# Router of a language-model kernel: the base rows move from VectorE to ScalarE, the root's inputs from GpSimd to VectorE

## Reference

```python
h = weight[x]                                   # token rows
h = h + attention(layernorm(h))                 # 16 heads, rotary terms
n = layernorm(h)                                # (h - mean) / sqrt(var + 1e-5)
probs = softmax(n @ w_router)                   # 32 experts, top 1
slot = expert * C + position of the token among its expert's, if below C = 320
y = expert(n)                                   # silu(n w_gate) * (n w_up) @ w_down
out = h + (n + y * gate)                        # the second n is the ffn block's own residual
```

## Time and profile before

| | |
|---|---|
| runs | 3315.01 us median of 3 (3313.55 to 3324.78) |
| profiled execution | 3315.87 us, span 3314.0 us |
| stage C | from 2914 to 3064 us of the span |
| PE / DVE / ACT / POOL busy over the span | 97% / 88% / 74% / 17% |
| mean granted TensorE clock | 0.986 of full speed |

### The profile page before, as it was taken

One profiled execution on the slowest core, in us unless ns is written; L12 is line 12 of the kernel. 1 busy time (PEld: TensorE's weight loads), 2 busy tenths in 40 slices (PEclk: granted clock), 3 DMA queues, 4 the chain that ended last, 5 costly groups with the idle time before them and its releaser, 6 DMA issues.

```text
span 3314.0 us, 67613 instructions
## 1 busy us (share of the span) xinstructions
PE 3202.7 (97%) x27520; PEld 1369.7 (41%) x27520; DVE 2908.6 (88%) x3157; ACT 2468.7 (74%) x4578; POOL 565.3 (17%) x752
## 2 busy tenths in 40 slices
PE   7997999999999999999999999999999999986999
PEld 3443333333333333333333333333333333365666
DVE  6889999999999999999999999999999999567222
ACT  3331888888888888888888888888888888943221
POOL 7882000000000000000000000000000000046233
PEclk9997999999999999999999999999999999998999
DMA  6895213131313131313131313122222220168773
GB/s 201 256 299 159 54 49 72 37 72 37 72 38 72 38 74 38 72 40 72 37 72 39 83 34 79 39 70 44 65 45 58 45 83 21 37 204 305 231 238 101
DMA packets 269155, 305.40 MB, mean 92 GB/s; under 512 B 45270, under 2 KB 198399, under 8 KB 265517
## 3 DMA queue, kind: packets, MB, share of 16 engines
q1 hardware_dynamic: 256812, 271.63, 29.7%
q0 software_dynamic: 12032, 29.45, 2.7%
HBM read 165.81 MB, written 139.23 MB: 92 GB/s over the span
## 4 chain that ended last, share of the span: by engine, by line
PE 81%; ACT 4%; DVE 3%; issue 2%; POOL 1%; DMA 0%; another core or an unknown queue 0%; SPq 0%; POOLq 0%; DVEq 0%
PE ps_o L916 33%; PE ps_s L899 26%; PE ps_m L868 13%; ACT probs L1012 2%; PE ps_g L1592 2%; PE ps_y L1603 2%; PE ps_u L1592 2%; DVE max_parts L1027 2%; ACT weighted L992 1%; PE ps_td L1581 1%; ACT rows_c L1343 1%; POOL slot_rows L1257 0%; PE ps_s L883 0%; POOL shift_c L1234 0%; DVE stats_c L1377 0%
## 5 line engine op out<-in xcount | busy, mean ns | idle before, releaser
L1027 DVE TENSOR_REDUCE max_parts<-ps_m 128x2 f32<-128x1024 f32 x2048 | 2486.1, 1223 | 79.9 <-PE ps_m L868 71.5
L1012 ACT ACTIVATE probs<-ps_s 128x512 f32<-128x512 f32 x4096 | 2217.5, 597 | 312.3 <-PE ps_s L899 127.8
L868 PE MATMUL ps_m<-keys,queries 48*128 48x512 f32 x4096 | 1483.5, 453 | 17.1 <-DVE max_parts L1027 16.7
L899 PE MATMUL ps_s<-queries,keys 51*128 51x512 f32 x4096 | 1480.5, 447 | 9.5 <-ACT probs L1012 3.1
L916 PE MATMUL ps_o<-probs,vals 128*32 128x256 f32 x16384 | 1295.5, 391 | 0.0
L899 PEld LDWEIGHTS ps_s<-queries,keys 51*128 51x128 f32 x4096 | 610.5, 185 | 832.2 <-issue 785.2
L868 PEld LDWEIGHTS ps_m<-keys,queries 48*128 48x128 f32 x4096 | 595.4, 187 | 77.4 <-DVE max_parts L1027 50.2
L916 PEld LDWEIGHTS ps_o<-probs,vals 128*32 128x32 f32 x16384 | 329.4, 108 | 720.4 <-issue 699.0
L824 POOL TENSOR_TENSOR heads_out<-weighted,recip_rows 128x512 f32<-128x512 f32 x63 | 80.9, 1285 | 2147.4 <-DMA recip_rows<-recip_rows_dram 2147.4
L1663 DVE TENSOR_TENSOR hidden<-ps_u,silu 128x320 f32<-128x320 f32 x64 | 31.5, 492 | 127.4 <-PE ps_u L1592 101.6
L1639 ACT ACTIVATE silu<-ps_g 128x320 f32<-128x320 f32 x64 | 28.0, 438 | 134.1 <-PE ps_g L1592 82.8
(11 more groups left out here) (108 smaller groups left out, 1600.0 us busy)
## 6 DMA issues: line engine op xcount, KB each, us to landing
slot_rows<-empty SPq DMA_DIRECT2D x16, 1290.0 KB, 5.2
vext<-val SPq DMA_DIRECT2D x64, 256.0 KB
halves_q<-parts SPq DMA_DIRECT2D x64, 256.0 KB
halves_k<-parts SPq DMA_DIRECT2D x64, 256.0 KB
keys<-halves_k SPq DMA_DIRECT2D x32, 512.0 KB, 7.5
queries<-halves_q SPq DMA_DIRECT2D x128, 128.0 KB, 3.2
vals<-vext SPq DMA_DIRECT2D x32, 512.0 KB, 5.6
recip_rows<-recip_rows_dram SPq DMA_DIRECT2D x64, 256.0 KB
```

The costliest lines, as they stand in the source:

```text
L868: mm = pe.matmul(ps_m[m % 2][:, h, :], queries_r[par][rows, qt, p, t * P:(t + 1) * P], keys_r[par][rows, p, c * 512:(c + 1) * 512], start= ...
L899: pe.matmul(ps_s[bank][:], keys_r[par][rows, p, k * P:(k + 1) * P], queries_r[par][rows, qt, p, :], start=True, stop=True).then_inc(scores ...
L1012: act.activation(probs[:, n % RING, :], ps_s[bank][:], ACT.Exp, scale=SCALE).then_inc(probs_ok[bank], 1)
L1027: dve.tensor_reduce(max_parts[:, lu % 2, :, p, t, c], ps_m[m % 2][:], AX.X, ALU.max).then_inc(maxima_ok[m % 2], 1)
```

## The change

1. Router, DVE: `base` is gone. After the gate, DVE makes `neg_mean` and `var_eps` by two `tensor_scalar` on 128x4 (`root_inputs`); the moments now come before the gate.
2. Router, ACT: a new `base` of four activations `resid * (rstd + 1) + shift`, which is `h + n`. It follows `normalise` of the next chunk.
3. Router, POOL: `root` loses `var_eps` and `neg_mean` and gains `rstd_one` = `rstd` + 1. The wait for the base rows stands ahead of `root`.
4. Router, DVE: since ACT now reads `resid` for the base, `residual` of chunk c + 2 waits until the base of chunk c is written.
5. Stage A: DVE makes `neg_mean` and `var_eps`, between the two `sums`; POOL's `root` loses them.

```diff
 (stage A)
@@ gpsimd, root
-                pool.wait_ge(stats_ok, after(b, k, CT))
-                pool.tensor_tensor(var_eps[:, k, :], mv[:, k, :, 1], eps_sb[:], ALU.add).then_inc(eps_ok, 1)
-                pool.tensor_tensor(neg_mean[:, k, :], no_mean[:], mv[:, k, :, 0], ALU.subtract).then_inc(neg_mean_ok, 1)
                 pool.wait_ge(eps_ok, after(b, k))
@@ vector
+            def root_inputs(b, k):
+                dve.wait_ge(stats_ok, after(b, k, CT))
+                dve.tensor_scalar(neg_mean[:, k, :], mv[:, k, :, 0], -1.0, None, ALU.mult)
+                dve.tensor_scalar(var_eps[:, k, :], mv[:, k, :, 1], EPS, None, ALU.add).then_inc(eps_ok, 1)
...
                 dve.tensor_tensor(sums[:, 1, 0, :], terms[:, 1, 0, :], terms[:, 1, 1, :], ALU.subtract).then_inc(sums_ok[1], 1)
+                if ahead:
+                    root_inputs(*ahead)
                 dve.tensor_tensor(sums[:, 1, 1, :], terms[:, 1, 2, :], terms[:, 1, 3, :], ALU.add).then_inc(sums_ok[1], 1)
 (router)
@@ sync, chunk
-                sp.wait_ge(base_ok, after(b, k))
+                sp.wait_ge(base_ok, after(b, k, CT))
@@ gpsimd, root
-                pool.wait_ge(stats_ok, after(b, k, CT))
-                pool.tensor_tensor(var_eps[:, k % 2, :], mv[:, k % 2, :, 1], eps_sb[:], ALU.add).then_inc(eps_ok, 1)
-                pool.tensor_tensor(neg_mean[:, k % 2, :], no_mean[:], mv[:, k % 2, :, 0], ALU.subtract).then_inc(neg_mean_ok, 1)
...
                 pool.tensor_tensor(shift[:, k % 2, :], neg_mean[:, k % 2, :], rstd[:, k % 2, :], ALU.mult).then_inc(shift_ok, 1)
+                pool.tensor_tensor(rstd_one[:, k % 2, :], rstd[:, k % 2, :], ones_c[:], ALU.add).then_inc(rstd_one_ok, 1)
@@ gpsimd, chunk
+                pool.wait_ge(base_ok, after(b, k, CT))
                 if not (last and k + 2 >= CPB):
                     root(*nxt(b, k, 2))
-                pool.wait_ge(base_ok, after(b, k))
@@ scalar
+            def base(b, k):
+                act.wait_ge(rstd_one_ok, after(b, k))
+                for t in range(CT):
+                    act.activation(rows[:, k, t, DM:2 * DM], resid[:, k % 2, t, :], ACT.Identity, bias=shift[:, k % 2, t:t + 1],
+                                   scale=rstd_one[:, k % 2, t:t + 1]).then_inc(base_ok, 1)
...
                     normalise(*nxt(b, k, 2))
+                if not (last and k == CPB - 1):
+                    base(*nxt(b, k))
 
             normalise(0, 0)
             copy_t(0, 0)
             normalise(0, 1)
+            base(0, 0)
@@ vector, residual
+                if (b, k) not in ((0, 0), (0, 1)):
+                    dve.wait_ge(base_ok, after(b, k, CT) - 2 * CT)
@@ vector
-            def base(b, k):
-
-                dve.wait_ge(norm_ok, after(b, k, CT))
-                dve.tensor_tensor(rows[:, k, :, DM:2 * DM], resid[:, k % 2], rows[:, k, :, 0:DM], ALU.add).then_inc(base_ok, 1)
+            def root_inputs(b, k):
+                dve.wait_ge(stats_ok, after(b, k, CT))
+                dve.tensor_scalar(neg_mean[:, k % 2, :], mv[:, k % 2, :, 0], -1.0, None, ALU.mult)
+                dve.tensor_scalar(var_eps[:, k % 2, :], mv[:, k % 2, :, 1], EPS, None, ALU.add).then_inc(eps_ok, 1)
@@ vector, chunk
+                if more:
+                    row_moments(*n)
                 gate(b, k)
                 if more:
-                    row_moments(*n)
+                    root_inputs(*n)
                 counts(b, k)
                 own(b, k)
                 slots(b, k)
-                if not (last and k == CPB - 1):
-                    base(*nxt(b, k))
```

More of the change, by code:

```diff
@@ L229, in phase_a @@
         neg_half = sb("neg_half", [P, CT])
-        eps_sb = sb("eps_sb", [P, CT])
-        no_mean = sb("no_mean", [P, CT])
         neg_mean = sb("neg_mean", [P, 4, CT])
@@ L255, in phase_a @@
         eps_ok = sem("eps_ok")
-        neg_mean_ok = sem("neg_mean_ok")
         rstd_ok = sem("rstd_ok")
@@ L368, in root @@
                 pool.wait_ge(rstd_ok, after(b, k))
-                pool.wait_ge(neg_mean_ok, after(b, k))
                 pool.tensor_tensor(shift[:, k, :], neg_mean[:, k, :], rstd[:, k, :], ALU.mult).then_inc(shift_ok, 1)
             pool.memset(neg_half[:], -0.5).then_inc(half_set, 1)
-            pool.memset(eps_sb[:], EPS).then_inc(half_set, 1)
-            pool.memset(no_mean[:], 0.0).then_inc(half_set, 1)
-            pool.wait_ge(half_set, 3)
+            pool.wait_ge(half_set, 1)
             for k in range(2):
@@ L569, in _ @@
             dve.memset(val[:], 1.0).then_inc(ones_set, 1)
-            row_stats(0, 0)
-            dve.wait_ge(stats_raw, CT)
-            row_moments(0, 0)
-            row_stats(0, 1)
-            dve.wait_ge(stats_raw, 2 * CT)
-            row_moments(0, 1)
+            for k in range(2):
+                row_stats(0, k)
+                dve.wait_ge(stats_raw, (k + 1) * CT)
+                row_moments(0, k)
+                root_inputs(0, k)
             dve.wait_ge(const_in, 16 * NCONST)
@@ L1108, in phase_c @@
         w_o, w_router, expert_no = router.w_o, router.w_router, router.expert_no
-        neg_half, eps_sb, no_mean, carry = router.neg_half, router.eps_sb, router.no_mean, router.carry
+        neg_half, carry = router.neg_half, router.carry
         token_no, att_t, emb = router.token_no, router.att_t, router.emb
@@ L1117, in phase_c @@
         shift = sb("shift_c", [P, 2, CT])
+        rstd_one = sb("rstd_one", [P, 2, CT])
+        ones_c = sb("ones_c", [P, CT])
         rows = sb("rows_c", [P, CPB, CT, ROW])
@@ L1149, in phase_c @@
         eps_ok = sem("eps_ok_c")
-        neg_mean_ok = sem("neg_mean_ok_c")
         rstd_ok = sem("rstd_ok_c")
         shift_ok = sem("shift_ok_c")
+        rstd_one_ok = sem("rstd_one_ok")
         norm_ok = sem("norm_ok_c")
@@ L1232, in root @@
                 pool.wait_ge(rstd_ok, after(b, k))
-                pool.wait_ge(neg_mean_ok, after(b, k))
                 pool.tensor_tensor(shift[:, k % 2, :], neg_mean[:, k % 2, :], rstd[:, k % 2, :], ALU.mult).then_inc(shift_ok, 1)
+                pool.tensor_tensor(rstd_one[:, k % 2, :], rstd[:, k % 2, :], ones_c[:], ALU.add).then_inc(rstd_one_ok, 1)
             pool.memset(neg_half[:], -0.5).then_inc(half_set, 1)
-            pool.memset(eps_sb[:], EPS).then_inc(half_set, 1)
-            pool.memset(no_mean[:], 0.0).then_inc(half_set, 1)
-            pool.wait_ge(half_set, 6)
+            pool.memset(ones_c[:], 1.0).then_inc(half_set, 1)
+            pool.wait_ge(half_set, 3)
             pool.wait_ge(proj_ps, 1)
@@ L1451, in _ @@
                 row_moments(0, k)
-            base(0, 0)
+                root_inputs(0, k)
             dve.wait_ge(carry_set, 1)
```

2 lines of the change are left out of this document (removed).

## The result

| | before | after |
|---|---|---|
| median of 6 runs each | 3314.28 us (3311.21 to 3324.78) | 3335.2 us (3332.89 to 3351.98) |
| profiled execution | 3315.87 us, span 3314.0 | 3332.89 us, span 3331.1 |
| mean granted TensorE clock | 0.986 | 0.983 |
| first stage, up to the last `full` | 284.1 | 284.4 |
| attention, up to the router's first residual add | 2634.2 | 2633.5 |

The ratio of the changed kernel to the one before is 1.007, with the interval 1.0049 to 1.009: slower, as forecast. Nearly all of it lies in the router, 16.8 of the 17.1 us between the two spans. The stage lengths are read from timelines of VectorE and TensorE.

A forecast was written before the change was run, and what follows sets the result against it. The router was taken as bound by a turn of waits, 8.04 us a chunk, becoming 9.30. Router 16.4 + 2.0 - 0.6 = 17.8 plus first stage 2.2 gave 20.0 us more: 3335.0 us, range 3325 to 3346.

The forecast's parts named there:

- The ring: Router, one turn a chunk: residual add, root inputs, GpSimd root, ScalarE normalisation and base, next residual add; 9.30 us against 8.04.
- Step 1: Router, VectorE from the start of the residual add through statistics, gate, moments and the two new instructions: 3.68 us.
- Step 2: Router, hand-over by semaphore from VectorE to GpSimd: 0.10 us, an estimate.
- Step 3: Router, GpSimd from the start of `rstd` to ScalarE's start: 1.35 us.
- Step 4: Router, ScalarE's eight activations in a row, normalising and base: 4.07 us.
- Step 5: Router, hand-over from ScalarE back to VectorE: 0.10 us.
- 13 x 1.26 = 16.4: Router, 13 turns, each longer by 9.30 - 8.04 us: 16.4 us more.
- The start: Router start: from the moments of chunk 1, the residual add of chunk 2 comes 2.0 us later.
- The end: Router end: last normalisation starts 5.13 us after its residual add instead of 5.70, 0.6 us back; the tail keeps its length.
- The first stage: First stage: two small VectorE instructions between the sums of the keys cost 0.16 us in each of 14 chunks, 2.2 us.
- Rival A: Router: the new wait does not bind, turn 7.50 us through the exponentials; 3310.2 us, no change to tell; chance 0.12.
- Rival B: Router: TensorE falls to its low clock and stays there, turn 11.5 us, 28.6 us more, 3363.6 us; chance 0.08.

The follow-up runs named there:

- second traces: The unchanged kernel before and the changed kernel each run and profiled once more: 3313.15 us and 3334.47 us, one run each.
- The doses: Changed kernel with two extra ScalarE activations a chunk, before (3362.13 us) or after the base rows (3343.19), or with half the residual add waiting for two rows (3325.93).
- dose in the ring: Changed kernel with two more activations a chunk on ScalarE, unused results, ahead of the four base activations: 3362.13 us, ratio 1.0142 to the kernel before.
- dose beside the ring: Changed kernel with two more activations a chunk on ScalarE, unused results, after the base rows and ahead of the copy: 3343.19 us, ratio 1.0093.
- router alone: Changed kernel with the first stage as before, its two small root inputs back on GpSimd: 3337.38 us, ratio 1.0068 to the kernel before.
- Inputs alone: Kernel before with only the router's root inputs made by VectorE, moments ahead of the gate, base add still on VectorE: 3313.32 us, ratio 0.9999.
- three buffers: Changed kernel with a third residual buffer, so the residual add of chunk c + 2 waits for the base of chunk c - 1: 3321.99 us, ratio 1.0019.
- base early: Changed kernel with ScalarE's base of chunk c + 1 ahead of the normalisation of chunk c + 2: 3320.29 us, ratio 1.0016 to the kernel before.

## Why the prediction was right

3335.0 us was forecast, 3335.2 measured. That the two agree to 0.2 us is luck: the spans of the two profiled executions lie 17.1 us apart, those of the second traces 21.5, and the medians 20.9. By its own steps:

- **The bound** was read rightly as a turn and not as the engine with the largest busy share. VectorE's busy share fell from 14.42 of 16 us to 12.71 of 18.56 and the stage became longer.
- **The ring.** Step 1, 3.68: measured 3.66. Step 2, the hand-over to GpSimd, 0.10: measured 0.15. Step 3, 1.35: 1.35. Step 4, 4.07: 4.04. Step 5, 0.10: 0.09. Sum 9.30 forecast, 9.29 in the turn shown, 9.28 as the mean of 13. The doses moved it by what they should. The wait itself was forecast as about 2.5 us in each of chunks 2 to 15; it is so in nine of them and smaller in five.
- **13 x 1.26 = 16.4.** The other side of the difference is less firm than it looked. The second trace of the kernel before has 7.87 us in nearly every turn and not 8.58 and 7.44 by turns, so the steady part costs 16.1 us in the first pair of traces and (9.31 - 7.89) x 13 = 18.5 in the second.
- **The start, +2.0.** From the moments of chunk 1 to the residual add of chunk 2 the changed kernel takes 2931.36 - 2925.17 = 6.19 us, against 4.21 in the earlier trace rows: 1.98 more. The mechanism is right, but in the first trace most of it was given back: the projection of chunk 1 ran at full clock there and the moments came earlier. TensorE, changed kernel, first trace:

```profile
2919.27 3.69 PE L1264 MATMUL ps_p<-w_o,att_t 128*128 128x256 f32 x16 [2.50 <-DVE resid L1375]
```

  and second trace:

```profile
2918.59 5.38 PE L1264 MATMUL ps_p<-w_o,att_t 128*128 128x256 f32 x16 [2.51 <-DVE resid L1375]
```

  In both traces of the kernel before it took 5.38. The granted clock from 2918 to 2926 us was 1.00 in the one and 0.79 in the three others, after the same idle time of 2.5 us. From the first residual add to that of chunk 2 the traces have 13.21 (before, twice), 13.51 and 15.19 (changed): +0.3 and +2.0. All 14 traces agree. The 16 matmuls took 3.69 us in seven of them and 5.29 to 5.38 in the other seven. Nine traces, in which the residual add of chunk 2 starts without a wait for base rows, have 13.2 us from the one add to the other with either. With the wait (and no dose in the ring) there are two more, 13.50 behind matmuls of 3.69 (dose beside the ring) and 15.17 behind the longer kind (router alone). So the term was right for a start with the longer matmuls, which the traced kernel before had, and 1.7 too high for the other.
- **The end, -0.6.** The last normalisation starts 3057.20 - 3052.04 = 5.16 us after its residual add, forecast 5.13, before 5.70. The logits of chunk 15 start at 3062.41, 3.14 us after that normalisation ended, as in the earlier trace rows.
- **Router together, +17.8:** measured +16.8 and +21.1, mean 19.0. With the first stage's 0.8, below, that makes 19.8 against 20.0 forecast; a router term 1.2 too small and a first-stage term 1.4 too large cancel, which is luck again.
- **The first stage, +2.2, was too high.** VectorE's first `sums` of the keys, changed kernel:

```profile
56.36 2.10 DVE L591 TENSOR_TENSOR sums<-terms 128x512 f32<-128x512 f32 x1
...
153.11 2.11 DVE L591 TENSOR_TENSOR sums<-terms 128x512 f32<-128x512 f32 x1
172.27 2.11 DVE L591 TENSOR_TENSOR sums<-terms 128x512 f32<-128x512 f32 x1
```

  Six spacings from 56.36 to 153.11 are 16.12 us each, where the kernel before has 16.00: 0.12 and not 0.16. The next is 19.16 where it was 19.55, since a transfer sets it, and the last two stages of the 14 do not have the step at all. From that block to the last one, the nine traces with this first stage have 223.7 to 225.3 us, the five without it 222.9 to 224.1: +0.8 on average. The term should have been some 0.8. Two of the 14 steps were none, the others 0.13 and not 0.16, and the spacing that a transfer sets gave 0.6 back (19.2 on average against 19.8), so the rival within the sum, that transfers swallow it, held for that part.
- **`shift`** took 0.19 to 0.20 in every chunk and not 0.85, and no base add of VectorE stands beside it now. Inputs alone shows how fine this is: `shift` took 0.21 us in the chunks where it started 0.06 ahead of the base add, and 1.27, up to the end of that add, in the three where it started 3 to 5 ns behind it. **`own_place`** took 0.29 beside a running `rstd` (2990.93, `rstd` from 2990.86 to 2991.90). The rule of the Trainium skill, page "SBUF — State Buffer", section "Who interferes with whom", would have it wait for the end of `rstd`, which issued first; the row does not show that, and neither does any other of the 14 chunks in which the two overlap. Nothing in the ring hung on it.
- **Rival A** did not come: the wait bound in all 14 chunks. Its consequence was tested by the kernels that took the wait away. Its price was 7.50 us a turn and no win. With three buffers the turns without a long wait for a load take 6.8 to 7.8 us, three of them 7.31; the means of 7.5 to 8.0 hold the late loads too. The time was the same as before or up to 0.2% longer.
- **Rival B** did not come. TensorE stood 2.00 us ahead of the projections and kept full clock in most turns. The low level appeared for single stretches. VectorE's slack took those that left the clock of a turn at 0.82, as the text said, but not the longer ones: behind a turn at 0.65 the next took 9.67 (changed kernel, second trace), and a turn at 0.54 took 10.06 (router alone). That is this rival in single turns, 0.4 to 0.9 us each, and 1.6 once with the dose in the ring. The Trainium skill, page "TensorE: Matmul & The Clock Gate", section "Why this matters for your kernels", advises against idle gaps between bursts of matmuls, and means longer ones than were needed here: the turn at 0.54 began with 2.00 us of idle TensorE, as did turns at full clock, and in the kernel with base early 2.54 us of waiting for a load was followed by 8 us at 0.50.

VectorE's share, 12.71 of 18.56, is 10.96 of 16, where some 11 was said.

## What to carry to other kernels

Moving work to an idle engine helps only if no ring that it comes to lie in gets longer than the present turn. Whoever lets another engine read a buffer gives the writer of that buffer a new wait: follow it once around, add the durations and hand-overs, and compare with the present turn. That sum was right to 0.02 us here, while the busy shares alone would have spoken for the change. The cheapest mends are to be sought in the wait itself: to wait for half a buffer gave back 0.68 of 1.24 us a turn without any memory, and another order on the freed engine gave back all.

When an edit of a small stage is judged, the totals are not enough: split the span by stages first. Here 5 us gained in the router were hidden by 4 us in a stage that no edit had touched. And before two traces of a stage are compared, see whether both started at the same clock: here that alone was 1.7 us.

## What was not expected of the hardware

- The attention steps, as a mean over 61, repeat within 0.02 us between two executions of one kernel (on two kernels), but differ between kernels that share this code: 40.40 to 40.54 us a step, 8.4 us over 61 of them. The cause is open.
- The same 16 matmuls after the same idle time of 2.50 us took 3.69 us in seven traces and 5.29 to 5.38 in the other seven; both come up with the same program.
- The step after the first stage took from 38.5 to 48.9 us with the granted clock, 10 us on the whole run.
- `own_place`, which reads two SBUF tensors, ran its usual 0.29 us beside `rstd` on GpSimd in all 14 chunks, though `rstd` had started 0.06 to 0.08 us before, while `shift` behind the start of the wide base add ended only when that add had, 0.85 or 1.27 us instead of 0.20 (the earlier trace rows and inputs alone).
